# The third PSUM slot goes back to the scores early in the second stretch, and one projection pair moves to a shared bank

## The chip, the cores and the metric

The kernel runs on one core of a Trainium2 chip. The metric is the device time of one execution, in microseconds. Three runs of the kernel before gave a median of 302.7 us (302.45 to 302.79). The engines are called PE (TensorE matmul), PEld (its weight loads), DVE (VectorE), ACT (ScalarE), POOL (GpSimd) and SP (the queue that issues transfers).

## The reference

One transformer layer over a sequence of 2048 rows of 128 features, in float32:

```python
x = x + attention(layernorm(x))      # 16 heads of 8, rotary embedding, causal mask, softmax, output projection
x = x + ffn(layernorm(x))            # base linear + shared low rank (16) + top 2 of 6 routed low-rank experts
```

In the attention, q, k and v come from one product with `w_qkv`; q and k are rotated (`x1*cos - x2*sin`, `x2*cos + x1*sin`), the scores are `q.k / sqrt(8)` for the keys up to the query's own row, and their softmax weights v.

## The kernel before

**Scores, exponentials, values.** The scores are made transposed (keys on partitions, queries along the free dimension), in 280 *units*. A unit is one PSUM slot of two banks (128x1024 float32), filled by four matmuls of 256 columns ("wide": two pairs of heads), four of 128 ("half": the last, diagonal key tile) or two of 512 ("full"). ACT takes the exponential of a whole unit from PSUM into one of eight buffers `pbuf` (L701), POOL masks the diagonal ones (L641), and PE multiplies a *block* of two units with the values (L1133, always 16 or 8 matmuls into the bank `po`). A block's value product stands `LAG` = 5 units behind its scores. When the last block of a group of four heads is done, DVE turns `po` into SBUF (L763, "evacuate"), and the next group's first value product waits for that (`o_free`).

**Stretches.** The queries are worked in six pieces. Units 0 to 7 are the first piece (query tiles 0, 1), units 8 to 23 the second (tiles 2, 3; four groups of wide, wide, wide, half), units 24 to 75 the third (tiles 4 to 7; 512 queries at a time), and so on. In text and code "the second stretch" is units 8 to 23.

**Side jobs.** Beside the attention of one piece, the engines prepare the next chunk of 512 rows: T (turn the normalised rows), Q and K (projections), QS and KS (the same with the halves of each head swapped, for the rotary term; only in the first chunks), V, B (sum for the bound), then the row's finish work. PE makes the products (L1149, L1155, L1161, L1184); `PRODUCTS_AT` says behind which unit each stands in PE's program. DVE takes Q and K with the cosine (L873), QS and KS with the sine (L876), adds the two (L788), and splits the sum into three bfloat16 parts (L796, L798, L805, L807) that SP stacks by DMA; `JOBS_AT` says behind which unit each stands in DVE's program. Every engine works strictly through its own written order, so an instruction that waits holds all that stand behind it on that engine.

**PSUM.** Eight banks: three slots of two banks (`ps`), `po`, and `pm`, the one bank of the side jobs. In the first two pieces the scores use only slots 0 and 1; the two banks of slot 2 serve as *spare banks* for chunk 2's Q, QS, K and KS (`SPARE_BANK`), and unit 24 is the first in slot 2. Unit u may be written once ACT has read the last unit in its slot; the first unit in the spare slot also waits until DVE has taken the last spare job:

```python
if LAST_IN_SLOT[u] is not None:
    pe.wait_ge(exp_ready, LAST_IN_SLOT[u] + 1)
if u == FIRST_IN_SPARE:
    pe.wait_ge(job_fed, FED[SPARE_READ])
```

A product job waits until DVE has taken the job before it in the same bank (`AWAITED`, through `job_fed`, which DVE raises with a small `engine_nop`, L932, behind the whole job). Two side products are read by ACT instead of DVE: T of chunk 2 (L671) and V of chunk 2 (L673), each placed in ACT's order behind the exponential of the unit in `ACT_PLACES`.

**PE's order around the change (before):** unit 8, values of block 1, **V**; unit 9, **K**; unit 10, block 2; unit 11, **KS**; unit 12, block 3; unit 13; unit 14, block 4; unit 15; unit 16, block 5; unit 17; unit 18, block 6; unit 19; unit 20, block 7, **B**; unit 21; unit 22, block 8; unit 23; unit 24, block 9. Blocks 4, 6, 8 and 10 are the first of their group, and blocks 3, 5, 7 and 9 the last of one. **DVE's order:** evacuate block 1, Q, QS, first split of Q, evacuate block 2 (in the first piece each group is a single block), second split of Q, evacuate block 3, K, KS, evacuate block 5, bound (L812 to L817), first split of K, evacuate block 7, flag (L821, L822), second split of K, evacuate block 9, evacuate block 11, and then the normalisation of chunk 3's rows, behind which PE's T of chunk 3 stands. Before unit 24, PE also loads a flag and branches on it (`row_maxima`, whose body did not run here).

Of the kernel before, what the change touches and what calls it, by code (L numbers as in the profile page):

```python
# [71 lines left out]
NS = 3  # L72
NS_SMALL = 2
# [25 lines left out]
def plan():  # L99


    units, blocks = [], []
    for i, (t0, tiles) in enumerate(PIECES):
        for g in range(NG):
            end = (i, g) == (NPIECE - 1, NG - 1)
            work = group_work(t0, tiles, end)
            if end:
                work[-1:] = [[unit] for unit in work[-1]]
            for n, members in enumerate(work):
                mine = list(range(len(units), len(units) + len(members)))  # L110
                for kind, kt, pairs in members:
                    units.append(dict(i=i, g=g, kind=kind, kt=kt, pairs=pairs, diagonal=kt >= t0, block=len(blocks)))
                blocks.append(dict(i=i, g=g, units=mine, first=n == 0, last=n == len(work) - 1,
                                   diagonal=any(units[u]["diagonal"] for u in mine)))
    return units, blocks


UNITS, BLOCKS = plan()
MASKS_THROUGH = [sum(u["diagonal"] for u in UNITS[:n + 1]) for n in range(len(UNITS))]
FIRST_UNIT = [next(n for n, u in enumerate(UNITS) if u["i"] == i) for i in range(NPIECE)]  # L120
SLOT = [u % NS_SMALL if u < FIRST_UNIT[2] else (u - FIRST_UNIT[2] - 1) % NS for u in range(len(UNITS))]
LAST_IN_SLOT = [next((v for v in range(u - 1, -1, -1) if SLOT[v] == SLOT[u]), None) for u in range(len(UNITS))]
FIRST_IN_SPARE = SLOT.index(NS_SMALL)
NEW_KEYS_UNIT = {next(n for n, u in enumerate(UNITS) if u["i"] == i and u["diagonal"]): p for i, p in NEW_PREP.items()}
# [25 lines left out]
def value_terms(block):  # L150
# [19 lines left out]
PRODUCT_JOBS = ("T", "Q", "QS", "K", "KS", "B", "V", "O", "X", "R", "U", "F")  # L170
INPUT_OF = {"T": "L3", "Q": "T", "K": "T", "V": "T", "B": "BD", "O": "A", "X": "M3", "R": "X", "U": "W2", "F": "U"}
READ_BY_ACT = (("T", 2), ("V", 2))
SPARE_BANK = {("Q", 2): 0, ("QS", 2): 1, ("K", 2): 0, ("KS", 2): 1}

LATE_FILLS = ([("Q", 0.0, 2 * TC + t) for t in range(TC)]
              + [("K", ONE_ONE, 3 * TC + t) for t in range(TC)] + [("Q", 0.0, 3 * TC + t) for t in range(TC)])
# [30 lines left out]

SMALL_PRODUCTS = (
    (("T", 2), ("Q", 2), ("B", 1), ("QS", 2)),
    (("V", 2), ("K", 2), ("KS", 2), ("B", 2)),  # L210
)
SMALL_PLACES = (
    (2, 4, 4, 7),
    (0, 1, 3, 12),
)
ACT_PLACES = (2, 9)
POOL_STACK_PLACE = 5


# [29 lines left out]
PRODUCTS_AT, PRODUCTS = products()  # L249
COPIES_AT = dict(zip(ACT_PLACES, READ_BY_ACT))  # L250
FULL = {job: sum(other not in READ_BY_ACT for other in PRODUCTS[:n + 1]) for n, job in enumerate(PRODUCTS)}


def awaited(job):


    name, c = job
    mine = SPARE_BANK.get(job)
    before = [other for other in PRODUCTS[:PRODUCTS.index(job)] if SPARE_BANK.get(other) == mine]
    needs = before[-1:] + ([(INPUT_OF[name], c)] if name in INPUT_OF else [])  # L260
    return max((JOB[need] for need in needs if need in JOB), default=None)


AWAITED = {job: awaited(job) for job in PRODUCTS}
SPARE_READ = max(JOB[job] for job in SPARE_BANK)
FEEDS = sorted({n for n in AWAITED.values() if n is not None} | {SPARE_READ})
# [3 lines left out]
def build(nc, x, w_qkv, rope_c, rope_s, w_out, w_down, w_up, w_base, router_b, ident, head_sum,  # L270
# [3 lines left out]
    with ExitStack() as ctx:  # L274
# [232 lines left out]
        def product_bank(name, c):  # L507

            spare = SPARE_BANK.get((name, c))
            return pm[:, :] if spare is None else ps[:, NS_SMALL, spare, :]  # L510
# [135 lines left out]
        def _(act):  # L646
# [47 lines left out]
            for u, unit in enumerate(UNITS):  # L694
                act.wait_ge(scores_ready, u + 1)
                if u >= NPB:
# [3 lines left out]
                probs = pbuf[:, u % NPB, :].rearrange("p (b q) -> p b q", b=2)  # L700
                nc.scalar.activation(probs[:, :, 0:width], ps[:, SLOT[u], :, 0:width],  # L701
                                     ACT.Exp, scale=SCALE).then_inc(exp_ready, 1)
# [392 lines left out]
        def _(pe):  # L1095
            def scores(u):
# [7 lines left out]
                for at, pair in enumerate(unit["pairs"]):  # L1104
                    for dk, q0, n, place in pieces(unit["kind"]):
# [3 lines left out]
                        for e in range(2):  # L1109
                            ins = nc.tensor.matmul(ps[:, SLOT[u], e, place:place + n],  # L1110
                                                   side(kst, e)[:, g * 2 + pair, key:key + P],
# [51 lines left out]
            def job(name, c):  # L1163

                if AWAITED[name, c] is not None:
                    pe.wait_ge(job_fed, FED[AWAITED[name, c]])
                product = product_bank(name, c)
                tile = lambda t: slice(t * P, (t + 1) * P)
                nt = FINISHES[c][1] if name in FINISH else TC
                if (name, c) == ("Q", 2):  # L1170
                    pe.wait_ge(second_read, 1)
                if (name, c) in (("QS", 2), ("K", 2)):
                    pe.wait_ge(second_read, 2)
                if name in ("Q", "QS", "K", "KS", "V") and c == 2:
                    pe.wait_ge(second_input, 1)
                if (name, c) == ("B", 1):
                    pe.wait_ge(second_input, 1)
                if (name, c) == ("B", 2):
                    pe.wait_ge(v_ready, 3)
                if name == "T":  # L1180
                    if c == 2:
                        pe.wait_ge(second_rows, TC)
                    for t in range(TC):
                        ins = nc.tensor.transpose(product[:, tile(t)], xn[:, chunk(c) % 2, t, :], idf[:, :])  # L1184
                elif name in ("K", "KS", "Q", "QS"):
                    ins = project(c, name, product)
                elif name == "V":
                    ins = project_v(c, product)
                elif name == "B":
                    ins = sum_bound(product)  # L1190
                elif name == "O":
                    pe.wait_ge(ffn_in, 16 * 5)
                    for t in range(nt):
                        ins = nc.tensor.matmul(product[:, tile(t)], feat[:, tile(t)], wout[:, :], start=True, stop=True)  # L1194
                elif name == "X":
                    for t in range(nt):
                        ins = nc.tensor.transpose(product[:, tile(t)], ln[:, t, :], idf[:, :])
                elif name == "R":
                    for t in range(nt):
                        ins = nc.tensor.matmul(product[:, t * P:t * P + RD + E], feat[:, tile(t)], wdown[:, :],  # L1200
                                               start=True, stop=True)
                elif name == "U":
                    for t in range(nt):
                        ins = nc.tensor.transpose(product[0:RD + 1, tile(t)], low_rank[:, t, 0:RD + 1], idf[:, :])  # L1204
                elif name == "F":
                    base(product, nt)
                    for t in range(nt):
                        ins = nc.tensor.matmul(product[:, tile(t)], lowT[0:RD + 1, t, :], wup[:, :], start=False, stop=True,  # L1208
                                               skip_group_check=True)
                ins.then_inc(act_full if (name, c) in READ_BY_ACT else job_full, 1)  # L1210
# [183 lines left out]
```

## Time and profile before

| | |
|---|---|
| median of 3 runs | 302.7 us (302.45 to 302.79) |
| profiled execution | 302.73 us, span 301.0 us |
| PE busy | 279.7 us, 93% |
| ACT busy | 267.3 us, 89% |
| DVE busy | 140.5 us, 47% |
| POOL busy | 65.9 us, 22% |
| granted TensorE clock | 1.00 throughout |

The profiled execution took 302.73 us, of which 301.0 us are the span from its first to its last instruction; about 1.7 us lie around it. The busy shares are averages over stages; which engine holds up which, in the stage of the change, has to be read from the order in time.

### The profile page before, as it was taken

The page shows a single profiled execution, that of the slowest core. Times are in us where ns is not written, and L with a number is a line of the kernel's source. Part 1 is how long each engine was busy: PE and PEld are TensorE (multiplying, and loading weights), DVE is VectorE, ACT ScalarE, POOL GpSimd, SP SyncE. Part 2 cuts the span into 40 slices and gives each one's busy share as a digit, 9 for nine tenths or more (in the row PEclk, how much of TensorE's full clock was granted, in tenths as well). Part 3 has the DMA queues.
Part 4 walks back from the last instruction along what each step waited for, and adds up shares of the span by engine and source line. Part 5 has one row for each costly group of instructions (what it writes and reads, how often), then busy time and mean ns, then how long its engine had stood idle before and what let it go on. Part 6 is the DMA issues. An engine that isn't in the chain of part 4 may idle for free.

```text
span 301.0 us, 7509 instructions
## 1 busy us (share of the span) xinstructions
PE 279.7 (93%) x3002; PEld 101.6 (34%) x3002; DVE 140.5 (47%) x422; ACT 267.3 (89%) x302; POOL 65.9 (22%) x144
## 2 busy tenths in 40 slices
PE   7969989998999899899999999999999999999995
PEld 2624332223334122132224124433533334433342
DVE  5876866688754767728421005551001514101064
ACT  8557899898997989999999999999999999999900
POOL 3576465413303004003030030101101010103000
PEclk9999999999999999999999999999999999999999
DMA  6343433006500100610000000000100000000000
GB/s 198 113 106 86 126 106 108 0 3 165 152 0 2 38 1 5 162 47 0 3 0 18 20 2 2 2 2 2 35 3 3 2 2 0 2 20 2 3 0 17
DMA packets 15256, 11.75 MB, mean 39 GB/s; under 512 B 2081, under 2 KB 14226, under 8 KB 15218
## 3 DMA queue, kind: packets, MB, share of 16 engines
q1 hardware_dynamic: 14594, 10.64, 12.8%
q8 instruction: 25, 0.41, 0.6%
q0 software_dynamic: 192, 0.39, 0.5%
q10 hardware_dynamic: 432, 0.20, 0.3%
q14 instruction: 13, 0.11, 0.1%
HBM read 3.88 MB, written 1.05 MB: 16 GB/s over the span
## 4 chain that ended last, share of the span: by engine, by line
PE 35%; ACT 27%; issue 16%; DVE 16%; DMA 2%; SPq 0%; ACTq 0%; DVEq 0%
ACT pbuf L701 27%; PE po L1133 16%; PE ps L1110 9%; DVE rest L781 3%; PE ps L1149 2%; PE pm L1149 1%; DMA qst<-parts 1%; DVE absmax L812 1%; PE pm L1143 1%; PE pm L1194 1%; PE pm L1155 1%; DMA xs<-x_dram 1%; DVE rot L775 1%; DVE rest L798 1%; PE pm L1208 1%
## 5 line engine op out<-in xcount | busy, mean ns | idle before, releaser
L701 ACT ACTIVATE pbuf<-ps 128x1024 f32<-128x1024 f32 (+1 forms) x280 | 254.0, 1092 | 15.0 <-PE ps L1110 14.3
L1133 PE MATMUL po<-pbuf,va 128*9 128x256 f32 (+3 forms) x1792 | 143.8, 426 | 2.6 <-ACT pbuf L701 1.4
L1110 PE MATMUL ps<-qst,kst 64*128 64x256 bf16 (+3 forms) x896 | 97.1, 297 | 7.5 <-ACT pbuf L701 3.6
L641 POOL TENSOR_SCALAR_AFFINE_SELECT pbuf<-pbuf 128x256 f32<-128x256 f32 (+1 forms) x104 | 48.2, 486 | 199.7 <-ACT pbuf L701 199.1
L1110 PEld LDWEIGHTS ps<-qst,kst 64*128 64x128 bf16 x896 | 29.6, 94 | 102.9 <-ACT pbuf L701 78.3
L1133 PEld LDWEIGHTS po<-pbuf,va 128*9 128x9 f32 x1792 | 35.2, 89 | 57.6 <-issue 35.8
L763 DVE STREAM_TRANSPOSE oq<-po 128x256 f32<-128x256 f32 (+1 forms) x24 | 12.9, 538 | 83.3 <-PE po L1133 83.0
L1256 PE MATMUL ps<-kst 128*128 128x512 bf16 x46 | 11.3, 380 | 1.0 <-issue 1.0
L781 DVE TENSOR_TENSOR rest<-pm,sinT 32x512 f32<-32x512 f32 x16 | 11.0, 687 | 0.3
L730 DVE BATCH_NORM_STATS2 stats<-xs 128x6 f32<-128x128 f32 x32 | 7.1, 281 | 3.2 <-DMA xs<-x_dram 1.7
L1149 PE MATMUL ps<-xnT,wqkv 128*128 128x256 f32 (+1 forms) x24 | 8.3, 470 | 0.2 <-ACT xnT L671 0.2
L926 DVE COPY lowT<-pm 113x512 f32<-113x512 f32 (+1 forms) x4 | 2.5, 624 | 12.5 <-PE pm L1204 12.5
L929 DVE TENSOR_TENSOR xs<-pm,xs 128x512 f32<-128x512 f32 (+1 forms) x4 | 2.5, 625 | 11.8 <-PE pm L1208 11.8
L1256 PE MATMUL ps<-xnT 128*128 128x512 bf16 x16 | 5.6, 530 | 1.5 <-DVE xnT L1044 1.5
L899 DVE TENSOR_TENSOR xs<-pm,xs 128x512 f32<-128x512 f32 (+1 forms) x4 | 2.5, 625 | 9.4 <-PE pm L1194 9.4
L1256 PEld LDWEIGHTS ps<-kst 128*128 128x128 bf16 x46 | 4.3, 99 | 5.6 <-issue 1.9
L600 POOL MEMSET qst<- 128x512 f32 (+1 forms) x9 | 6.0, 692 | 0.0
L788 DVE TENSOR_TENSOR rot<-rot,rest 128x512 f32<-128x512 f32 (+1 forms) x10 | 5.9, 585 | 0.3
L798 DVE TENSOR_TENSOR rest<-rot,parts 128x512 f32<-128x512 f32 (+1 forms) x8 | 5.6, 702 | 0.3
L649 ACT COPY kst<-fillers 128x2048 f32<-128x2048 f32 x3 | 5.7, 1897 | 0.0
L775 DVE TENSOR_TENSOR rot<-pm,cosT 128x512 f32<-128x512 f32 x4 | 2.8, 692 | 6.0 <-PE pm L1149 5.1
L807 DVE TENSOR_TENSOR parts<-rest,parts 128x512 bf16<-128x512 f32 (+1 forms) x8 | 5.2, 645 | 0.3
(154 smaller groups left out, 178.7 us busy)
## 6 DMA issues: line engine op xcount, KB each, us to landing
qst<-parts SPq DMA_DIRECT2D x18, 128.0 KB, 2.5
kst<-parts SPq DMA_DIRECT2D x18, 128.0 KB, 2.5
xs<-x_dram SPq DMA_DIRECT2D x4, 256.0 KB, 3.8
cosT<-rope_c_dram SPq DMA_DIRECT2D x3, 256.0 KB, 4.0
sinT<-rope_s_dram SPq DMA_DIRECT2D x3, 256.0 KB, 5.0
out_dram<-xs SPq DMA_DIRECT2D x3, 256.0 KB, 2.3
kst<-parts SPq DMA_DIRECT2D x8, 64.0 KB, 2.2
qst<-parts SPq DMA_DIRECT2D x7, 64.0 KB, 2.5
```

Of the source, the lines that this page charges most:

```text
L600: nc.gpsimd.memset(stacked[:, :, first * P:(first + tiles) * P].bitcast(F32), value).then_inc(filled_by_pool, 1)
L641: ins = nc.gpsimd.affine_select(out=edge, in_=edge, compare_op=ALU.is_ge, fill=0.0, base=0, pattern=[[0, edge.shape[1]], [1, P]], channel_ ...
L701: nc.scalar.activation(probs[:, :, 0:width], ps[:, SLOT[u], :, 0:width], ACT.Exp, scale=SCALE).then_inc(exp_ready, 1)
L730: ins = nc.vector.bn_stats(stats[:, t, :], xs[:, tile + t, :])
L763: nc.vector.transpose(oq[:, g, mine, :].rearrange("p b r -> p (b r)"), po[:, 0:nt * P]).then_inc(o_free, 1)
L781: ins = nc.vector.tensor_tensor(rest[there:there + HALF, which, cols], product[here:here + HALF, :], sinT[here:here + HALF, c % 2, cols], ...
L788: return nc.vector.tensor_tensor(rot[:, which, cols], rot[:, which, cols], rest[:, which, cols], ALU.add)
L798: then(nc.vector.tensor_tensor(rest[:, which, cols], rot[:, which, cols], parts[:, which, 0, cols], ALU.subtract))
L1110: ins = nc.tensor.matmul(ps[:, SLOT[u], e, place:place + n], side(kst, e)[:, g * 2 + pair, key:key + P], side(qst, e)[:, g * 2 + pair, q:q ...
L1133: ins = nc.tensor.matmul(po[32 * j:32 * j + DH + 1, q0:q0 + n], va[:, kt, g * GH + j, :], pbuf[:, u % NPB, at:at + n], start=blk["first"] ...
L1149: return nc.tensor.matmul(product, wqkv[:, which, :], xnT[:, chunk(p) % 2, local(p)], start=True, stop=True)
L1256: nc.tensor.matmul(into, left, right, start=True, stop=True)
```

## The change

Slot 2 serves the scores from unit 10 on instead of unit 24, and so the rotation over three slots begins 14 units earlier. Of the spare banks only Q and QS remain; K and KS of chunk 2 go through `pm`, the bank that T, B and V use too, one after the other. In PE's order K stays behind unit 9, KS goes from behind unit 11 to behind unit 14, and V from behind unit 8 to behind unit 18. ACT's copy of V moves from behind the exponential of unit 9 to behind that of unit 18. DVE's order is untouched.

```diff
-SLOT = [u % NS_SMALL if u < FIRST_UNIT[2] else (u - FIRST_UNIT[2] - 1) % NS for u in range(len(UNITS))]
+BACK = FIRST_UNIT[1] + 2
+SLOT = [u % NS_SMALL if u < BACK else (u - BACK - 1) % NS for u in range(len(UNITS))]
...
-SPARE_BANK = {("Q", 2): 0, ("QS", 2): 1, ("K", 2): 0, ("KS", 2): 1}
+SPARE_BANK = {("Q", 2): 0, ("QS", 2): 1}
...
 SMALL_PRODUCTS = (
     (("T", 2), ("Q", 2), ("B", 1), ("QS", 2)),
-    (("V", 2), ("K", 2), ("KS", 2), ("B", 2)),
+    (("K", 2), ("KS", 2), ("V", 2), ("B", 2)),
 )
 SMALL_PLACES = (
     (2, 4, 4, 7),
-    (0, 1, 3, 12),
+    (1, 6, 10, 12),
 )
-ACT_PLACES = (2, 9)
+ACT_PLACES = (2, 18)
...
                 if (name, c) == ("Q", 2):
                     pe.wait_ge(second_read, 1)
-                if (name, c) in (("QS", 2), ("K", 2)):
+                if (name, c) == ("QS", 2):
                     pe.wait_ge(second_read, 2)
```

Through the tables, unit 10 (`FIRST_IN_SPARE`) now waits for DVE to have taken QS (`SPARE_READ`), K waits for DVE's flag job of chunk 1, KS for DVE's K, and V for DVE's KS. The last 256 units rotate over the three slots as before, one step shifted.

## Rows read from the trace of the kernel before

**Rows 1.** The page: busy time, then shares of the chain that ended last.
```profile
PE 279.7 (93%) x3002; PEld 101.6 (34%) x3002; DVE 140.5 (47%) x422; ACT 267.3 (89%) x302; POOL 65.9 (22%) x144
...
PE 35%; ACT 27%; issue 16%; DVE 16%; DMA 2%; SPq 0%; ACTq 0%; DVEq 0%
```
**Rows 2.** ACT in order of time, units 9 to 36: start, duration, count, idle before.
```profile
28.59 1.02 ACT L701 ACTIVATE pbuf<-ps 128x1024 f32<-128x1024 f32 x1 [1.16 <-PE ps L1110]
29.51 0.58 ACT L673 COPY va<-pm 128x512 f32<-128x512 f32 x1
29.98 1.58 ACT L701 ACTIVATE pbuf<-ps 128x1024 f32<-128x1024 f32 x2
32.35 10.61 ACT L701 ACTIVATE pbuf<-ps 128x1024 f32<-128x1024 f32 x12 [0.78 <-PE ps L1110]
43.15 12.24 ACT L701 ACTIVATE pbuf<-ps 128x1024 f32<-128x1024 f32 x13 [0.19 <-PE ps L1110]
```
**Rows 3.** PE in order of time, from V behind unit 8 to T of chunk 3.
```profile
27.07 1.16 PE L1155 MATMUL pm<-wqkv,xnT 128*128 128x128 f32 x8
28.16 0.39 PE L1110 MATMUL ps<-qst,kst 64*128 64x256 bf16 x4
...
29.55 0.39 PE L1110 MATMUL ps<-qst,kst 64*128 64x256 bf16 x4
...
30.86 1.13 PE L1149 MATMUL ps<-xnT,wqkv 128*128 128x512 f32 x2
31.91 0.39 PE L1110 MATMUL ps<-qst,kst 64*128 64x256 bf16 x4
...
33.75 1.05 PE L1133 MATMUL po<-pbuf,va 128*9 128x256 f32 x16
34.74 0.29 PE L1110 MATMUL ps<-qst,kst 64*128 64x128 bf16 x4
35.44 0.39 PE L1110 MATMUL ps<-qst,kst 64*128 64x256 bf16 x4 [0.41 <-ACT pbuf L701]
...
37.27 1.05 PE L1133 MATMUL po<-pbuf,va 128*9 128x256 f32 x16
...
38.95 0.39 PE L1110 MATMUL ps<-qst,kst 64*128 64x256 bf16 x4 [0.41 <-ACT pbuf L701]
...
41.05 1.05 PE L1133 MATMUL po<-pbuf,va 128*9 128x256 f32 x16 [0.20 <-DVE oq L763]
...
42.73 0.39 PE L1110 MATMUL ps<-qst,kst 64*128 64x512 bf16 x2 [0.40 <-issue]
...
53.34 0.66 PE L1184 MATMUL pm<-idf,xn 128*128 128x128 f32 x4 [0.82 <-DVEq L932]
```
**Rows 4.** DVE in order of time, from the evacuation of block 1 to that of block 11.
```profile
27.21 0.45 DVE L763 STREAM_TRANSPOSE oq<-po 128x256 f32<-128x256 f32 x1 [1.20 <-PE po L1133]
...
29.14 0.69 DVE L788 TENSOR_TENSOR rot<-rot,rest 128x512 f32<-128x512 f32 x1
...
33.14 0.45 DVE L763 STREAM_TRANSPOSE oq<-po 128x256 f32<-128x256 f32 x1
33.63 0.69 DVE L873 TENSOR_TENSOR rot<-ps,cosT 128x512 f32<-128x512 f32 x1
34.35 0.69 DVE L876 TENSOR_TENSOR rest<-ps,sinT 128x512 f32<-128x512 f32 x1
...
36.66 0.45 DVE L763 STREAM_TRANSPOSE oq<-po 128x256 f32<-128x256 f32 x1 [0.90 <-PE po L1133]
...
40.46 0.45 DVE L763 STREAM_TRANSPOSE oq<-po 128x256 f32<-128x256 f32 x1
...
47.05 0.45 DVE L763 STREAM_TRANSPOSE oq<-po 128x256 f32<-128x256 f32 x1 [2.64 <-PE po L1133]
```
**Rows 5.** Busy time by engine in two windows: PE, PEld, DVE, ACT, POOL, granted clock, DMA.
```profile
27.07:33.75 6.68, 6.65 (x72) 2.92 (x68) 6.05 (x11) 4.68 (x7) 2.87 (x7) 1.00 0.37 92
33.75:42.73 8.98, 7.52 (x121) 2.96 (x120) 7.14 (x14) 8.82 (x11) 3.84 (x7) 1.00 0.40 107
```

## The prediction

> **What bounds the kernel now.** I read the page first. PE is busy for 93% of the span and ACT for 89%, and the chain that ended last passes through PE (35%), ACT (27%) and DVE (16%) [rows 1]. No single engine is the bound, so the question for each microsecond is which hand-over ends last in the stretch that the change touches. The change touches units 9 to 24 only; behind unit 24 the same three-slot rotation runs in both kernels. So I read the timelines of ACT, PE and DVE from 27 to 54 us, side by side, and placed each matmul group in the program by counting units and blocks.
>
> The ACT timeline tempts one to see a slot problem. ACT starts unit 9 after 1.16 us of idle time and unit 12 (at 32.35) after 0.78 us, then runs twelve and thirteen exponentials almost without a gap [rows 2]. The PE timeline shows waits for a slot too: 0.41 us before unit 16 (35.44) and 0.41 us before unit 20 (38.95), both released by an exponential [rows 3].
>
> The PE timeline also shows why ACT idled earlier. From 27.07 to 33.75 PE is busy for 6.65 of 6.68 us [rows 5]: V stands between units 8 and 9, K between 9 and 10, KS between 11 and 12. Those idle times of ACT are not a lack of slots. They are PE's side jobs.
>
> DVE is the third reader. From the evacuation of block 1 at 27.21 to the end of KS's sine product at 34.35 + 0.69 = 35.04 it is all but unbroken (6.05 of the first 6.68 us [rows 5], and no row of it begins with a wait for PE after the first) [rows 4]: Q, QS, the first split of Q, evacuation of block 2, the second split, evacuation of block 3 (33.14), K, KS. Nothing in that row of work waits on what the change moves, except KS at its end. So **the evacuation of block 3 stays at 33.14 in either kernel**, and so does the earliest start of block 4's value product, the first of the next group: 33.14 + 0.45 = 33.59, plus the hand-over. What the hand-over from an evacuation to PE costs shows at block 8: that of block 7 ends at 40.46 + 0.45 = 40.91 [rows 4], and PE, which waited for it, starts at 41.05 [rows 3], 0.14 us later. That gives 33.73. Before, block 4 started at 33.75 [rows 3]. PE reached it just as DVE allowed it.
>
> **The change part by part, as a pinned point and a sum behind it.**
>
> *Ahead of 33.75.* V leaves the place behind unit 8 (start to start 28.16 − 27.07 = 1.09 us) and KS the place behind unit 11 (31.91 − 30.86 = 1.05 us) [rows 3]. PE gets 2.14 us free there. Unit 9 starts 1.09 us sooner, at about 27.1, and K ends at about 28.5. Then comes the added wait: unit 10 needs slot 2, which DVE gives back when QS is added up and the small instruction behind it has run. The addition ends at 29.14 + 0.69 = 29.83 [rows 4]; a hand-over by that instruction is about as long as the 0.14 us above. So unit 10 starts at about 29.95 to 30.0, against 29.55 before: **1.4 us of new waiting on PE, and unit 10 is 0.4 us later than now**. Behind the waiting unit stand the value product of block 2 and unit 11, all 0.4 us late. With KS gone from there, unit 12 follows unit 10 by 31.91 − 29.55 − 1.05 = 1.31 us [rows 3] and starts at about 31.3, 0.6 us sooner. Blocks 3 and 4 then wait for the evacuations of blocks 2 and 3, and block 4 starts at 33.73. All of the 2.14 us is spent in waits for DVE: 1.4 us at unit 10 and the remaining 0.7 us at those two blocks. The gain at the pinned point is nothing.
>
> *ACT ahead of that point.* ACT may start unit 12 about 0.4 us sooner (31.9 instead of 32.35 [rows 2]). It does not last, because unit 15 stands behind KS.
>
> *From 33.75 to unit 24.* Before, this took 42.73 − 33.75 = 8.98 us, of which PE was busy for 7.52 [rows 5], so 1.46 us were idle. Of these, 0.40 us before unit 24 is the flag and its branch ("issue" [rows 3]); it stays. The rest, 1.06 us, is what later work can fill: 0.41 + 0.41 + 0.20 us of listed waits [rows 3] and crumbs. Into this window come KS (behind unit 14) and V (behind unit 18): 1.05 + 1.09 = 2.14 us. So unit 24 is late by 2.14 − 1.06 = **1.08 us**.
>
> *What else waits in that window.* KS needs DVE to have read K: 33.63 + 0.69 = 34.32 [rows 4], plus the hand-over, before block 4 ends at 34.74; no wait. DVE now waits for KS's product: it ends at about 35.8 (34.74 + 1.05), so the sine product starts 1.5 us later than 34.35, and the addition, as long as that at 29.14 (0.69 us [rows 4]), ends at about 37.3. The evacuation of block 5 is queued behind it: 37.3 to 37.8 instead of 36.66 to 37.1. Block 6's product waits for that, until about 37.9. PE by itself gets there at 35.8 + (37.27 − 34.74 − 0.41) = 37.9 as well [rows 3]. Value taken: 0.05 us, between 0 (DVE in time) and 0.4 (the sine product, the addition and the evacuation each a little longer than its row). The first split of K, the flag and the second split of K stand behind that evacuation on DVE, late by as much as PE is.
>
> *ACT's copy of V.* At 29.51 it cost nothing: it ended about when unit 10's scores were ready (29.98) [rows 2]. Now ACT reaches it behind unit 18's exponential, at about 39.4, but V's product ends only near 40.0. ACT waits about 0.6 us, copies for 0.5 us (29.98 − 29.51), and starts unit 19 at about 40.6. From there to unit 24 it needs two halves and three full exponentials: three at 0.90 to 0.94 us (12.24 us for thirteen [rows 2]) and two at about 0.6 us (a full and a half one took 1.58 us from 29.98), so it could start unit 24 at about 44.6. PE gives unit 24 at 43.9 + 0.4 = 44.3. So ACT would be 1.4 us late at unit 24, PE and DVE 1.1. ACT's surplus is worked off if PE or DVE sets the next point. In the trace of before that point is T of chunk 3 at 53.34, for which PE waited 0.82 us on DVE [rows 3], and DVE's work for it starts with the evacuation of block 11 at 47.05, which waited 2.64 us for PE [rows 4]. So the chain goes PE, DVE, PE, and ACT's lag is covered.
>
> *The third slot itself.* Before, it would have been worth the two waits of 0.41 us. In the changed order PE arrives at units 16 and 20 later than their slots come free even with two slots, because KS and V stand ahead of them. I count it at nothing beyond the 1.06 us already filled.
>
> *Sum.* 0 ahead of the pinned point, +2.14 for KS and V, −1.06 for idle time filled, +0.05 for block 6's wait: about **+1.1 us** at unit 24, carried by PE and DVE into everything behind it. The profiled execution took 302.73 us against a median of 302.7, so the sum may be set on either: 302.7 + 1.1 = **303.8 us**. The case's own range is 303.4 to 304.0.
>
> The Trainium skill (Perfetto Trace Analysis, section Matmuls under Optimizing Tensor Performance) says that independent matmul groups should rotate through different PSUM banks, so that the evacuation of one overlaps the next one's matmuls. By that rule K and KS in one bank should cost a wait. Here the row of K's read on DVE says that this costs nothing while KS stands behind block 4; what costs is where it stands.
>
> **The rivals.**
>
> *Faster: the slots were what mattered (302.1 us).* If ACT's own pace set the end of the window, the third slot would let it run at that pace. Twelve exponentials took 10.61 us, 3.54 us for each group of four [rows 2]; three full ones at 0.94 us and a half at 0.6 us are 3.42 us or less, some 0.12 to 0.2 us less for each of three groups. With unit 12 0.45 us sooner and the copy of V 0.5 us in ACT's way the net is 0.3 to 0.6 us. For it speaks that ACT is busy for 8.82 of 8.98 us in that window [rows 5]. Against it: it holds only from the point where PE can take 2.14 us more work in a window in which it idles 1.06 us. The Trainium skill (Perfetto Trace Analysis, section Optimization Strategy) says that the same gap, repeated, can mean that there isn't enough PSUM; by that rule the two gaps of 0.41 us ask for this very slot, and it would come out faster. The trace agrees that the gaps are slot waits, but they are what hides half of the moved work.
>
> *About the same: the delay is absorbed behind unit 24 (302.2 to 303.3, say 302.9).* PE's score pairs wait for slots again from 47 us on, and ACT runs thirteen exponentials unbroken from 43.15 [rows 2]. If ACT's own backlog, rather than its start, set T of chunk 3, part of 1.1 us would vanish; likewise if two hand-overs ahead of it had slack. Against it: unit 24's exponential waited 0.19 us for PE [rows 2], and DVE's chain to T starts with a wait for PE. The moment PE slips, all three slip.
>
> *Slower still: ACT carries its lag on (304.1 to 304.6, say 304.2).* If V's product comes later than I reckon, or T doesn't cover ACT's 1.4 us, the copy is in the chain in full.
>
> **How the numbers follow.** The forecast's case has 0.50, the absorbed one 0.19, the faster one 0.13, the one still slower 0.18. What a measurement of this kernel can tell from no change is about 0.2%, 0.6 us. The absorbed case falls mostly within that, a small part of it below or above. So: faster 0.12, same 0.18, slower 0.70. From 302.6 to 304.4 the range holds the forecast's case, most of the slower one and most of the absorbed one, a little over 0.8.
>
> **What the changed profile would show.** On PE: unit 9 near 27.1, then a gap of about 1.4 us released by DVE before unit 10 at 29.9 to 30.0; block 4 still at 33.7 to 33.8 with a wait for the evacuation; no waits of 0.41 us for exponentials before units 16 and 20; unit 24 near 43.9. On DVE: the evacuation of block 3 unchanged at 33.1, a wait of about 1.5 us for KS's product, that of block 11 at about 48.2. On ACT: about 1.2 us of idle time before unit 15 and some 0.6 before the copy of V. T of chunk 3 would be near 54.5. The prediction is wrong if block 4 starts well before 33.7, which means that DVE was not the pin, or if unit 24 is late by 1.1 us and the gap between the kernels closes later.

## The result and the profile after

The changed kernel takes **304.11 us** (median of 8 runs, 303.45 to 304.98) against 302.51 us for the kernel before (8 runs, 302.28 to 302.97). The ratio is 1.0052 with a 95% interval of 1.0035 to 1.0068, so it is slower by 0.5%, about 1.6 us. The forecast was 303.8 us, in a range of 302.6 to 304.4.

The profiled execution took 304.20 us with a span of 302.5 us. Its first exponential starts at 19.02 us, against 19.12 before. The profiled executions of this document differ by half a microsecond either way at that point (18.55 to 19.69), ahead of anything the edits touch. So below "late" and "early" mean: against the kernel before, once the start of unit 0's exponential is made equal in both.

PE in order of time, start, duration, count and idle time before, the rows that answer to [rows 3]:

```profile
26.96 0.39 PE L1111 MATMUL ps<-qst,kst 64*128 64x256 bf16 x4
27.28 1.12 PE L1150 MATMUL pm<-xnT,wqkv 128*128 128x512 f32 x2
29.92 0.39 PE L1111 MATMUL ps<-qst,kst 64*128 64x256 bf16 x4 [1.51 <-DVEq L933]
...
31.82 0.84 PE L1134 MATMUL po<-pbuf,va 128*9 128x256 f32 x16 [0.30 <-DVE oq L764]
...
33.67 1.05 PE L1134 MATMUL po<-pbuf,va 128*9 128x256 f32 x16 [0.47 <-DVE oq L764]
34.65 1.13 PE L1150 MATMUL pm<-xnT,wqkv 128*128 128x512 f32 x2
...
37.87 1.05 PE L1134 MATMUL po<-pbuf,va 128*9 128x256 f32 x16 [0.34 <-DVE oq L764]
38.85 1.16 PE L1156 MATMUL pm<-wqkv,xnT 128*128 128x128 f32 x8
...
41.95 1.05 PE L1134 MATMUL po<-pbuf,va 128*9 128x256 f32 x16 [0.17 <-DVE oq L764]
...
43.71 0.39 PE L1111 MATMUL ps<-qst,kst 64*128 64x512 bf16 x2 [0.49 <-issue]
...
54.80 0.65 PE L1185 MATMUL pm<-idf,xn 128*128 128x128 f32 x4 [1.29 <-DVEq L933]
```

Unit 9 starts at 26.96 and is 1.10 us early, and K follows; then PE stands idle for 1.51 us until DVE has given slot 2 back (29.92). Block 4's product, at 33.67, has waited 0.47 us for the evacuation of block 3: the pinned point is where it was (33.75 before). The two 0.41 us waits for a slot are gone, and KS (34.65) and V (38.85) stand in their place. Block 6's product (37.87) now waits 0.34 us for the evacuation of block 5. Unit 24 starts at 43.71 instead of 42.73, which with the 0.10 us of the start is **1.08 us late** (1.09 in the unrounded times).

DVE, the rows that answer to [rows 4]:

```profile
33.09 0.44 DVE L764 STREAM_TRANSPOSE oq<-po 128x256 f32<-128x256 f32 x1
33.56 0.69 DVE L874 TENSOR_TENSOR rot<-pm,cosT 128x512 f32<-128x512 f32 x1
35.82 0.69 DVE L877 TENSOR_TENSOR rest<-pm,sinT 128x512 f32<-128x512 f32 x1 [1.56 <-PE pm L1150]
...
37.28 0.45 DVE L764 STREAM_TRANSPOSE oq<-po 128x256 f32<-128x256 f32 x1
...
41.35 0.45 DVE L764 STREAM_TRANSPOSE oq<-po 128x256 f32<-128x256 f32 x1 [0.26 <-PE po L1134]
...
48.17 0.45 DVE L764 STREAM_TRANSPOSE oq<-po 128x256 f32<-128x256 f32 x1 [2.78 <-PE po L1134]
```

ACT, the rows that answer to [rows 2]:

```profile
36.04 3.35 ACT L702 ACTIVATE pbuf<-ps 128x512 f32<-128x512 f32 x4 [1.07 <-PE ps L1111]
40.05 0.59 ACT L674 COPY va<-pm 128x512 f32<-128x512 f32 x1 [0.66 <-PE pm L1156]
40.53 14.90 ACT L702 ACTIVATE pbuf<-ps 128x512 f32<-128x512 f32 x17
```

The windows that answer to [rows 5] (PE, PEld, DVE, ACT, POOL busy, clock, DMA):

```profile
27.00:33.67 6.67, 4.39 (x62) 1.80 (x59) 5.98 (x11) 4.50 (x6) 3.29 (x7) 1.00 0.48 125
33.67:43.71 10.04, 9.03 (x129) 4.44 (x129) 7.21 (x14) 8.30 (x11) 3.19 (x6) 1.00 0.31 82
```

Ahead of the pinned point PE is now busy for 4.39 of 6.67 us; 2.26 us of work have left and nothing has come sooner for it. Behind it PE is busy for 9.03 us where it was 7.52. ACT has no idle time between its copy of V and T of chunk 3 (seventeen exponentials in one row, from 40.53): it reaches unit 24 at its own pace, 1.16 us late, just behind PE.

Behind unit 24 a second, smaller loss appears. T of chunk 3 starts at 54.80 instead of 53.34, so it is 1.56 us late. From there to the last exponential nothing is gained or lost.

### The profile page after: what moved, and what is told of

It is laid out like the page before. It is cut to its first block, busy times and chain, and to the rows that moved or that the text cites. A ratio compares the mean times of both kernels' runs of the same rounds, so it can differ in the third digit from the quotient of the medians.

```text
span 302.5 us, 7509 instructions
## 1 busy us (share of the span) xinstructions
PE 278.9 (92%) x3002; PEld 102.0 (34%) x3002; DVE 141.2 (47%) x422; ACT 267.0 (88%) x302; POOL 66.1 (22%) x144
## 3 DMA queue, kind: packets, MB, share of 16 engines
HBM read 3.88 MB, written 1.05 MB: 16 GB/s over the span
## 4 chain that ended last, share of the span: by engine, by line
PE 34%; ACT 27%; issue 16%; DVE 16%; DMA 3%; POOL 1%; SPq 1%; ACTq 0%; DVEq 0%; POOLq 0%
ACT pbuf L702 27%; PE po L1134 16%; PE ps L1111 9%; DVE rest L782 3%; PE pm L1150 2%; DMA xs<-x_dram 2%; DVE rot L789 1%; DMA kst<-parts 1%; DVE oq L764 1%; PE pm L1195 1%; PE pm L1156 1%; PE pm L1144 1%; PE pm L1209 1%; DVE absmax L813 1%; DVE stats L731 1%
## 5 line engine op out<-in xcount | busy, mean ns | idle before, releaser
L1111 PE MATMUL ps<-qst,kst 64*128 64x256 bf16 (+3 forms) x896 | 95.8, 297 | 8.0 <-ACT pbuf L702 2.8
L1150 PE MATMUL pm<-xnT,wqkv 128*128 128x512 f32 x12 | 6.8, 645 | 0.2 <-DVEq L933 0.2
L1150 PE MATMUL ps<-xnT,wqkv 128*128 128x256 f32 (+1 forms) x20 | 6.1, 434 | 0.2 <-ACT xnT L672 0.2
```

What stands on the lines that cost most here:

```text
L1111: ins = nc.tensor.matmul(ps[:, SLOT[u], e, place:place + n], side(kst, e)[:, g * 2 + pair, key:key + P], side(qst, e)[:, g * 2 + pair, q:q ...
L1150: return nc.tensor.matmul(product, wqkv[:, which, :], xnT[:, chunk(p) % 2, local(p)], start=True, stop=True)
```

## The experiments

This table holds, for each profiled execution, how late PE's first matmul of unit 24, the exponential of unit 24 and the last exponential (unit 279) start (counted from the unrounded trace), and the times of all runs. Where ACT's figure for unit 24 is the later one, ACT was behind PE there. Ratios are to runs of the kernel before on the same chips.

| run | unit 24, PE | unit 24, ACT | last | median us (lowest to highest, runs) | ratio (interval) |
|---|---|---|---|---|---|
| changed kernel | +1.09 | +1.16 | +1.58 | 304.11 (303.45 to 304.98, 8) | 1.0052 (1.0035 to 1.0068) |
| after_again | +1.09 | +1.16 | +1.98 | 304.46 (303.67 to 305.43, 6) | 1.0057 (1.0041 to 1.0072) |
| after_warm | +0.94 | +1.16 | +1.00 | 303.76 (303.15 to 304.12, 5) | 1.0032 (1.0020 to 1.0044) |
| moves_only | +2.80 | +2.80 | +2.82 | 305.09 (304.0 to 306.11, 6) | 1.0074 (1.0051 to 1.0098) |
| slot_at_18 | −0.15 | −0.15 | −0.10 | 302.46 (302.07 to 303.88, 12) | 0.9997 (0.9985 to 1.0010) |
| before_v_late | +0.98 | +0.98 | +1.89 | 304.36 (303.18 to 306.26, 9) | 1.0051 (1.0031 to 1.0072) |
| v_back | +0.93 | +0.93 | +0.95 | 303.80 (303.23 to 304.38, 6) | 1.0038 (1.0025 to 1.0051) |
| v_back_swap | −0.08 | +0.20 | +0.69 | 304.80 (303.31 to 307.37, 6) | 1.0077 (1.0041 to 1.0112) |
| v_back_swap_x | −0.08 | +0.21 | +0.29 | 302.78 (302.31 to 303.54, 12) | 1.0006 (0.9997 to 1.0016) |
| after_swap_x | +0.86 | +1.16 | +1.22 | 303.62 (303.4 to 303.9, 5) | 1.0035 (1.0022 to 1.0049) |
| slot18_swap | −1.15 | −0.71 | +2.21 | 302.67 (301.96 to 305.05, 6) | 1.0014 (0.9985 to 1.0044) |
| slot18_swap_x | −1.14 | −0.71 | −1.17 | 301.85 (301.23 to 302.21, 12) | 0.9970 (0.9957 to 0.9983) |
| reordered_x | −1.78 | −1.35 | −1.29 | 301.41 (300.66 to 302.67, 12) | 0.9958 (0.9946 to 0.9970) |

**The moves without the slot.** The changed kernel, scores on two slots to unit 23:

```diff
-SLOT = [u % NS_SMALL if u < BACK else (u - BACK - 1) % NS for u in range(len(UNITS))]
+SLOT = [u % NS_SMALL if u < FIRST_UNIT[2] else (u - FIRST_UNIT[2] - 1) % NS for u in range(len(UNITS))]
```

> The changed kernel with the scores kept on two slots up to unit 23 (slot 2 idle from QS to unit 24); K, KS and V stand where the change puts them. Theory of the prediction (the moved products cost, the third slot is worth nothing there): unit 24 starts 1.1 us later than in the kernel before, as in the changed one, 303.6 to 304.1 us. Theory that the third slot hides part of the moved work: PE waits for slots at units 18, 20 and 22 again, unit 24 is late by about 1.7 us, 304.3 to 304.9 us. Rival that the slot itself hurts (its wait before unit 10 is what costs): with that wait gone unit 24 is late by under 0.5 us, 302.9 us.

Unit 24 was 2.80 us late, more than any theory had it. The profile shows two things: waits for a slot, as the second theory has it, and a stretch at half the clock. From the timeline of PE in this run, then its windows (the granted clock is the third number from the end):

```profile
31.56 1.07 PE L1133 MATMUL po<-pbuf,va 128*9 128x256 f32 x16 [1.66 <-POOL pbuf L641]
...
33.52 1.90 PE L1133 MATMUL po<-pbuf,va 128*9 128x256 f32 x16
...
42.89 0.39 PE L1110 MATMUL ps<-qst,kst 64*128 64x256 bf16 x4 [0.52 <-ACT pbuf L701]
```
```profile
29.00:31.00 2.00, 0.76 (x16) 0.23 (x8) 1.72 (x4) 1.96 (x3) 1.48 (x2) 1.00 0.28 69
31.00:33.00 2.00, 1.44 (x22) 0.73 (x24) 1.86 (x4) 0.00 (x0) 0.55 (x2) 0.76 0.70 184
33.00:35.00 2.00, 2.00 (x22) 0.56 (x18) 0.81 (x2) 1.79 (x2) 0.00 (x0) 0.50 0.52 140
35.00:37.00 2.00, 2.00 (x18) 0.67 (x18) 0.46 (x1) 0.38 (x2) 0.63 (x1) 0.89 0.38 109
```

PE had idled 1.66 us ahead of block 3, and then block 4's product took 1.90 us at a granted clock of 0.50 (1.2 GHz) instead of 1.05 at 1.00. Four of this kernel's six executions had a mean clock of 0.992; the two at 1.000 took 304.0 and 304.1 us. An estimate of what the clock took: the evacuation of block 3 ends at 33.12 and its hand-over takes 0.14 us, so block 4 could have started at 33.26; at the full clock it and KS behind it take 0.98 + 1.06 = 2.04 us, to 35.30, and the next scores started at 36.44. That is about 1.1 us of the 2.80, and the 1.7 us left are the second theory's number. The times don't confirm it: the two executions at full clock are within 0.3 us of the changed kernel's ten (median 303.88). So whether the third slot hides some of the moved work in this order stays open.

**The slot without the moves.** The kernel before, slot 2 back at unit 18:

```diff
-SLOT = [u % NS_SMALL if u < FIRST_UNIT[2] else (u - FIRST_UNIT[2] - 1) % NS for u in range(len(UNITS))]
+BACK = 18
+SLOT = [u % NS_SMALL if u < BACK else (u - BACK - 1) % NS for u in range(len(UNITS))]
```

> The kernel before with one edit: slot 2 returns at unit 18, after KS has been taken from it; no product moves. Theory that DVE pins block 8 (the evacuation of block 7 stands behind the first split of K on DVE): PE's 0.41 us wait before unit 20 goes, block 8 still starts at 41.0 to 41.1, unit 24 at 42.7, time unchanged at 302.5 us. Rival that slots were what mattered: unit 24 and the total are 0.4 us earlier, 302.1 us.

No change (0.9985 to 1.0010). The wait before unit 20 went and came back one step on, for the evacuation of block 7. PE, then DVE:

```profile
41.63 1.05 PE L1134 MATMUL po<-pbuf,va 128*9 128x256 f32 x16 [0.98 <-DVE oq L764]
```
```profile
40.00 1.00 DVE L799 TENSOR_TENSOR rest<-rot,parts 128x512 f32<-128x512 f32 x1
41.03 0.45 DVE L764 STREAM_TRANSPOSE oq<-po 128x256 f32<-128x256 f32 x1
```

The evacuation stands right behind the split of K in DVE's order. A slot wait of 0.41 us had stood ahead of a DVE wait and hidden it. Unit 24 came only 0.15 us early in the profile, because the "issue" time ahead of it was 0.25 us here and 0.40 before.

**V alone.** The kernel before with V and its copy at unit 18:

```diff
-    (("V", 2), ("K", 2), ("KS", 2), ("B", 2)),
+    (("K", 2), ("KS", 2), ("V", 2), ("B", 2)),
...
-    (0, 1, 3, 12),
+    (1, 3, 10, 12),
...
-ACT_PLACES = (2, 9)
+ACT_PLACES = (2, 18)
```

> The kernel before with V alone moved as in the change (product behind unit 18, ACT's copy behind the exponential of unit 18), K and KS in the spare banks, two slots. Theory of a sum over moved work: block 4 stays at 33.75, V's 1.09 us meets about 0.65 us of idle time behind unit 18, and ACT's copy comes on top: unit 24 late by 0.8 to 0.9 us with ACT starting unit 19 1.2 us late, 303.4 us. Rival that only KS matters (through DVE): unit 24 late by 0.2 us or less, 302.6 us.

Unit 24 was 0.98 us late, near the 0.8 to 0.9 of the sum; block 8 was 0.77 us late, and the "issue" time before unit 24 was 0.62 us instead of 0.40. Another 0.9 us came between units 32 and 36, on the way to T of chunk 3, of which more below.

**V undone, KS still late.**

```diff
-    (("K", 2), ("KS", 2), ("V", 2), ("B", 2)),
+    (("V", 2), ("K", 2), ("KS", 2), ("B", 2)),
...
-    (1, 6, 10, 12),
+    (0, 2, 6, 12),
...
-ACT_PLACES = (2, 18)
+ACT_PLACES = (2, 9)
...
-                if (name, c) == ("B", 2):
+                if (name, c) in (("K", 2), ("B", 2)):
                     pe.wait_ge(v_ready, 3)
```

> The changed kernel with V back behind unit 8 and its copy behind the exponential of unit 9, K behind unit 10 (it now waits for ACT's copy of V out of the shared bank), KS behind unit 14, third slot from unit 10. Theory of the prediction's sum (PE's moved time is what costs): only KS's 1.05 us is left to fill 1.06 us of idle time, so unit 24 is late by 0.4 us or less, 302.6 to 302.9 us. Rival, a chain through DVE (KS late, so evacuations of blocks 5 and 7 late behind the addition, the bound and the first split of K): unit 24 is late by about 1.1 us although V is back, 303.6 us.

The theory that PE's moved time is all that costs fell here: with V's 1.09 us back in its cover, unit 24 was still 0.93 us late. PE now idled for 1.12 us ahead of block 8. The row names ACT, but ACT's last exponential was long done; the evacuation of block 7 on DVE ended at 41.17 + 0.45 = 41.62, 0.15 us ahead of PE's start. PE, then DVE:

```profile
41.77 1.05 PE L1134 MATMUL po<-pbuf,va 128*9 128x256 f32 x16 [1.12 <-ACT pbuf L702]
```
```profile
33.04 0.45 DVE L764 STREAM_TRANSPOSE oq<-po 128x256 f32<-128x256 f32 x1 [0.33 <-PE po L1134]
...
35.78 0.69 DVE L877 TENSOR_TENSOR rest<-pm,sinT 128x512 f32<-128x512 f32 x1 [1.57 <-PE pm L1150]
...
40.37 0.77 DVE L799 TENSOR_TENSOR rest<-rot,parts 128x512 f32<-128x512 f32 x1
41.17 0.45 DVE L764 STREAM_TRANSPOSE oq<-po 128x256 f32<-128x256 f32 x1
```

KS is late, so DVE idles 1.57 us; addition, evacuation of block 5, bound and the first split of K are all late behind it, and the evacuation of block 7 stands behind them, 1.19 us late. Not all of that is the changed kernel's: here K stands behind unit 10, so the evacuation of block 3 is itself 0.38 us late (0.05 in the changed kernel). In the changed kernel the evacuation of block 7 is 1.00 us late and had waited 0.26 us for PE, so DVE's chain alone would have had it 0.74 us late.

**That chain undone as well.** On top of v_back, on DVE:

```diff
-SECOND = ("Q", "QS", "Q1", "Q2", "K", "KS", "BD", "K1", "B", "K2")
+SECOND = ("Q", "QS", "Q1", "Q2", "K", "KS", "BD", "B", "K1", "K2")
...
-    (0, 1, 1, 3, 5, 6, 9, 10, 14, 15),
+    (0, 1, 1, 3, 5, 6, 9, 12, 12, 15),
```

> The kernel of the run v_back with one more edit, on DVE: the flag and the first split of K stand behind the evacuation of block 7 instead of the split ahead of it. Theory of the chain through DVE: block 8's wait for that evacuation (1.12 us in v_back) shrinks to 0.4 us or less and unit 24 is late by 0.4 us instead of 0.9 to 1.1, 303.0 us. Rival that PE's own added work sets unit 24 there: no change against v_back, 303.6 to 303.8 us.

Unit 24 was 0.20 us late, and PE's wait of 1.12 us before block 8 was 0.10: what held block 8 in v_back was DVE's order. The total got worse all the same: in the profile DVE waited 0.76 us for the next chunk's rows, and three of the six executions had a mean clock of 0.986 to 0.994 and took 305.31 to 307.37 us. The next kernel is slot_at_18 with the same edit on DVE.

> The kernel before with slot 2 back at unit 18 (as in slot_at_18, which alone changed nothing) and on DVE the flag and the first split of K behind the evacuation of block 7. Theory that slot and DVE order pin block 8 together: PE's wait before unit 20 and the one before block 8 both go, unit 24 is 0.6 to 0.7 us earlier, 301.9 to 302.1 us. Rival that ACT's pace sets unit 24: 0.2 us or less, 302.4 us.

Here unit 24 came 0.71 us early, and in the profiled execution the end came 2.21 us late. Splits of K that end later let SP issue the loads behind them later, and DVE then waited for the rows of the next chunk. DVE, PE and the windows of slot18_swap:

```profile
49.10 0.87 DVE L731 BATCH_NORM_STATS2 stats<-xs 128x6 f32<-128x128 f32 x4 [1.16 <-DMA xs<-x_dram]
```
```profile
54.31 0.66 PE L1185 MATMUL pm<-idf,xn 128*128 128x128 f32 x4 [2.56 <-DVEq L933]
...
55.39 1.90 PE L1134 MATMUL po<-pbuf,va 128*9 128x512 f32 x8
```
```profile
51.50:55.00 3.50, 0.94 (x10) 0.52 (x8) 2.53 (x9) 2.17 (x3) 3.23 (x8) 1.00 0.00 0
55.00:57.00 2.00, 2.00 (x12) 0.14 (x10) 0.69 (x1) 1.02 (x1) 0.41 (x1) 0.50 0.00 0
57.00:59.00 2.00, 2.00 (x8) 0.62 (x6) 0.04 (x1) 0.00 (x0) 0.23 (x1) 0.65 0.00 0
```

One late load cost DVE 1.16 us and PE a wait of 2.56 us, and a stretch at half clock came behind it. The six executions fall in two groups: three with a mean clock of 0.994 took 303.31 to 305.05 us, three at 0.997 or more took 301.96 to 302.03, so their median says little. The following kernels therefore also load the rows ahead of the stacking on SP, an edit of one line. slot18_swap_x and v_back_swap_x are the two kernels above with it; after_swap_x is the changed kernel with it and the edit on DVE:

```diff
+            load_rows(2)
             stack(2)
-            load_rows(2)
```

> The kernel of slot18_swap, with one more edit on SP: the rows of the next chunk are loaded ahead of the stacking of chunk 2 instead of behind it. In slot18_swap unit 24 came 0.7 us sooner, but DVE then waited 1.16 us for those rows, T of chunk 3 came late and PE's wait of 2.56 us for it was followed by a stretch at the lower clock. Theory that the late load took the gain away: DVE has no such wait, T of chunk 3 is 0.6 to 0.9 us earlier than in the kernel before, 301.6 to 301.9 us. Rival that the stretch behind unit 24 gives the gain back in another way: 302.3 us or more.

0.9970 (0.9957 to 0.9983). With the load in time, the slot (put where no product has to move for it) and the order on DVE together gain 0.8 us. What that order and the load would gain without the slot was not run.

> The kernel of v_back_swap (the changed kernel with V back behind unit 8, K behind unit 10, and DVE's flag and first split of K behind the evacuation of block 7) with the rows loaded ahead of the stacking. Theory that with both chains undone only crumbs of the change's loss are left: unit 24 late by 0.1 to 0.4 us as in v_back_swap (0.2), no wait of DVE for rows, 302.6 to 303.0 us; the wait ahead of unit 10 (1.5 us) now and then costs the clock. Rival that the slot from unit 10 is a loss by itself: 303.3 us or more.

1.0006 (0.9997 to 1.0016): V back in its place, DVE's order changed, the third slot from unit 10 on, and the time is that of the kernel before. That doesn't show the slot at unit 10 to be free. slot18_swap_x has the same order on DVE and the same load, and there they gain; against it, this kernel is 0.9 us later at unit 24 (+0.21 against −0.71) and 0.9 us slower (302.78 against 301.85). K and KS late in the shared bank, with the slot from unit 10, still cost that much, and the edits on DVE and SP pay it back. Which of the two, the slot or the products, takes it was not separated.

> The changed kernel with only the chain through DVE undone: the flag and the first split of K behind the evacuation of block 7, rows loaded ahead of the stacking; V stays behind unit 18. Theory that either chain alone holds unit 24 back (PE's moved products here, DVE's late evacuation in v_back): unit 24 late by 1.1 to 1.2 us as in the changed kernel, 303.7 to 304.2 us. Rival that DVE's chain is the whole cause: unit 24 late by 0.2 us as in v_back_swap, 302.8 us.

The exponential of unit 24 was 1.16 us late, as in the changed kernel, but PE was not: its block 8 was 0.93 us late (1.00 in the changed kernel) and its unit 24 was 0.86 (1.09), of which 0.17 is a shorter "issue" time. What holds the exponential at 1.16 is ACT, which waits for the late V and then has no gap. PE, then ACT:

```profile
41.65 1.05 PE L1134 MATMUL po<-pbuf,va 128*9 128x256 f32 x16
...
43.24 0.39 PE L1111 MATMUL ps<-qst,kst 64*128 64x512 bf16 x2 [0.33 <-issue]
```
```profile
39.82 0.59 ACT L674 COPY va<-pm 128x512 f32<-128x512 f32 x1 [0.66 <-PE pm L1156]
40.30 14.84 ACT L702 ACTIVATE pbuf<-ps 128x512 f32<-128x512 f32 x17
```

So with DVE's chain undone, PE's moved products still make PE 0.9 us late, and ACT's wait for V makes ACT 1.16 us late.

**The idle time filled.** Is the clock part of the changed kernel's loss? Ten matmuls in the wait before unit 10:

```diff
-FEEDS = sorted({n for n in AWAITED.values() if n is not None} | {SPARE_READ})
+FEEDS = sorted({n for n in AWAITED.values() if n is not None} | {SPARE_READ, JOB["Q", 2]})
...
+                if u == FIRST_IN_SPARE:
+                    pe.wait_ge(job_fed, FED[JOB["Q", 2]])
+                    keep_warm(10, kst[:, 0, 0:P], kst[:, 0, 0:2 * P], ps[:, NS_SMALL, 0, 0:2 * P])
```

> The changed kernel once more, beside the next one. Its first eight times lay between 303.45 and 304.98 us, and two of the three highest had a mean granted clock of 0.992 or 0.994. Expected: 304.1 us again, with some executions at a clock below 0.996, and these the slowest.

> The changed kernel with ten matmuls of 256 columns put into PE's wait ahead of unit 10 (on keys that are long there, into the bank from which DVE has read Q, after it has). They add no result and leave the order alone; the wait for QS stays as long. Theory that PE's idle time there now and then costs it the full clock: all executions show a granted clock of 0.996 or more, the highest times go, the median falls by 0.2 to 0.6 us to 303.5 to 303.9 us. Rival that the clock has no part: the same median and spread as the changed kernel beside it.

The changed kernel beside it took 304.46 us; of its fourteen executions in all, four had a mean clock of 0.992 or 0.994, and they took 304.56, 304.65, 304.98 and 305.43 us. With the wait filled, five executions all showed 0.998 or more and none took over 304.12 us. PE in that run:

```profile
28.50 1.26 PE L1257 MATMUL ps<-kst 128*128 128x256 bf16 x10
30.04 0.40 PE L1111 MATMUL ps<-qst,kst 64*128 64x256 bf16 x4 [0.28 <-DVEq L933]
```

The exponential of unit 24 was 1.16 us late as ever, and block 8 1.00, so the order in which work waits is the same up to there. The lower clock is gone from all five executions. What that is worth in time is not clear of noise: 1.0032 (1.0020 to 1.0044) against 1.0057 (1.0041 to 1.0072) beside it and 1.0052 (1.0035 to 1.0068) before, and the ten executions of the changed kernel at 0.999 or more had a median of 303.88 us, close to the 303.76 here.

**The order that follows from it.** The kernel before with slot 2 back at unit 18, V behind unit 9, K behind 10, KS behind 13, the rows loaded ahead of the stacking, and on DVE K ahead of the second split of Q, and the flag and the first split of K behind the evacuation of block 7 (the lines for slot and load are those shown above):

```diff
-SECOND = ("Q", "QS", "Q1", "Q2", "K", "KS", "BD", "K1", "B", "K2")
+SECOND = ("Q", "QS", "Q1", "K", "Q2", "KS", "BD", "B", "K1", "K2")
...
-    (0, 1, 1, 3, 5, 6, 9, 10, 14, 15),
+    (0, 0, 2, 3, 6, 6, 8, 13, 13, 14),
...
-    (0, 1, 3, 12),
+    (1, 2, 5, 12),
...
-ACT_PLACES = (2, 9)
+ACT_PLACES = (2, 10)
```

> The kernel before, reordered around its waits: slot 2 back at unit 18, V behind unit 9, K behind unit 10, KS behind unit 13 (K and KS still in the spare banks), DVE takes K ahead of the second split of Q, the flag and the first split of K stand behind the evacuation of block 7, rows loaded ahead of the stacking. Theory (a replay of the order with the durations of the rows): unit 24 and T of chunk 3 are 0.9 to 1.2 us earlier, 301.4 to 301.8 us. Rival that ACT's pace and the evacuations leave nothing: 302.3 us or more.

301.41 us, 0.9958 (0.9946 to 0.9970), faster than both kernels by 1.2 and 2.7 us. KS, at 31.73 us, fits ahead of block 4's product, which starts at 33.11 and, with its start made equal, 0.16 us sooner than before. From its PE timeline:

```profile
31.73 1.12 PE L1150 MATMUL ps<-xnT,wqkv 128*128 128x512 f32 x2
...
33.11 1.05 PE L1134 MATMUL po<-pbuf,va 128*9 128x256 f32 x16
```

## Why the prediction was right, and where not

*The pinned point.* Right. Evacuation of block 3 at 33.09 (forecast 33.14), block 4 at 33.67 (33.73), both with the waits named: 1.51 us before unit 10 (forecast 1.4), then 0.30 and 0.47 us.

*The sum to unit 24.* Right in size: 1.08 us late on PE against 1.08 plus 0.05. KS and V took 1.06 and 1.09 us (34.65 to 35.71, 38.85 to 39.94). The other terms were off and cancelled, which is luck. From start to start, units 15 and 16 took 0.44 us instead of 1.02, units 19 and 20 0.43 instead of 1.03 and units 21 and 22 0.78 instead of 0.98: 1.38 us of waiting filled, not 1.06. Against that stands block 6's wait: units 17 and 18 ahead of it took 0.95 us instead of 0.74, so it cost 0.21 and not 0.05 (the row shows 0.34 us of idle time). And the "issue" time before unit 24, which "stays" in the prediction, was 0.49 instead of 0.40; over all runs it lay between 0.13 and 0.62, and no run shows why. DVE's wait for KS was 1.56 us (forecast 1.5), ACT's waits 1.07 and 0.66 us (1.2 and 0.6).

*What causes it.* Right for the changed kernel, but the prediction saw only a part of what stands beside it. It put the delay down to PE's work moved out of its cover and gave KS's way through DVE 0.05 us. PE's path is the one that ends last in the changed kernel: the evacuation of block 7 waited 0.26 us for PE there, and with DVE's order changed (after_swap_x) PE's block 8 is still 0.93 us late instead of 1.00. V alone makes unit 24 0.98 us late (before_v_late). Close behind PE run two more chains. DVE's evacuations behind a late KS would have block 8 about 0.74 us late (1.00 less 0.26), and in v_back, where K and KS are read later still, they make unit 24 0.93 us late (0.20 when the DVE order is changed). ACT, behind the late V, is 1.16 us late at unit 24 in both kernels. The three give 1.1 to 1.2 us, not the sum, because they run side by side. The step that failed is "the first split of K, the flag and the second split of K stand behind that evacuation on DVE, late by as much as PE is": I followed DVE to the evacuation of block 5 and not on to that of block 7. It did no harm to the number, because PE's path was 0.26 us longer.

*The third slot counted at nothing.* Not settled for units 11 to 23 of the changed order: moves_only lost much more in its profile, but with the lower clock in it. Less an estimate for the clock it would be 1.7 us late at unit 24, 0.6 more than the changed kernel, while its two executions at full clock (304.0 and 304.13 us) were within 0.3 us of the changed kernel's at full clock. In the order of before the slot alone is worth nothing (slot_at_18), as its wait hides another.

*Carried to the end.* The last exponential was 1.58 us late, not 1.1. The missing term is the way from unit 24 to T of chunk 3. PE reached block 11 late by a further 0.14 us, and DVE's chain behind it was 0.33 us longer than before. Its last rows, before and then after:

```profile
51.75 0.16 DVE L457 SCALAR_TENSOR_TENSOR rstd<-sq,rstd 128x4 f32<-128x4 f32 x1
51.94 1.29 DVE L471 TENSOR_SCALAR xn<-xs,mv,rstd 128x128 f32<-128x128 f32 x4
```
```profile
52.88 0.28 DVE L458 SCALAR_TENSOR_TENSOR rstd<-sq,rstd 128x4 f32<-128x4 f32 x1
53.20 1.49 DVE L472 TENSOR_SCALAR xn<-xs,mv,rstd 128x128 f32<-128x128 f32 x4
```

The extra between unit 24 on PE and T of chunk 3 was 0.46 us here, 0.87 in after_again and 0.06 in after_warm, all of them the same order of work, so it is not a fixed price of the change; and it is as large in before_v_late (0.87). What lengthens DVE's rows stays open. POOL's fills and masks run beside all four normalisations in both kernels (from 51.76 to 53.70 before, from 52.74 on after), so the overlap as such doesn't explain the difference; where in each row they fall may, and no edit tests it. The gap before block 11 was 0.37 us in after_again and 0.36 in before_v_late, and the profile puts it down to "issue", with nothing it waits for; its cause stays open too.

*The rivals.* "Faster" needed PE to absorb 2.14 us of work, which it couldn't. The Trainium skill (Perfetto Trace Analysis, section Optimization Strategy) reads a repeated gap as a possible lack of PSUM: slot_at_18 took one of the gaps away and the time stayed (0.9997); with DVE's order changed too, and the load ahead, the kernel was faster (0.9970). "Slower still" had ACT's lag as its mechanism; ACT was 1.16 us late at unit 24 (forecast 1.4) and 1.09 at unit 28, no more than DVE at the evacuation of block 9 (1.09), so it was covered as forecast, and the measured 304.1 us came near that rival's time for other reasons.

*The clock* was in no term. It was lower in four of fourteen executions, the profiled ones not among them. The medians of 304.11 and 304.46 us stand against 303.88 for the ten executions at full clock and 303.76 for after_warm: an estimate of 0.2 to 0.4 us, not clear of noise. The forecast of 303.8 us is 0.3 us off the median, but its step of 1.1 us is 0.5 off the measured 1.6: the kernel before took 302.51 us in these runs, not the 302.7 it was set on. Of the 0.5 us, 0.46 is the way to T in the profiled execution.

## What to carry to other kernels

When a product is moved, follow both ways on from it: the engine that makes it, and every instruction queued behind its reader, up to the next point where the first engine waits for the second. Chains that run side by side don't add up, and undoing one shows little; undo both before calling either harmless, and read each engine's own start at the point where they meet, because one engine's marker can stand still while another moves. When an edit undoes a delay, give the same edit to a kernel without the delay as well: it may be a gain of its own. A buffer that removes a wait pays only if no other wait stands right behind it, and a work item that ends later on the splitting engine may hold back a load queued on SP for a later stage.

## What the runs showed of the hardware that was not expected

Two waits of PE were followed by the lower of its clock's two levels (granted 0.50, 1.2 GHz): 1.66 us in moves_only, where a block of sixteen matmuls then took 1.90 instead of 1.05 us, and 2.56 us in slot18_swap. But other waits as long as the first were not. After 1.51 us in the profiled execution of the changed kernel, and after 1.69, 1.70 and 1.69 us before T of chunk 3 in after_again, before_v_late and v_back_swap, the clock stayed at 1.00. From after_again, the wait and the windows around it:

```profile
55.11 0.66 PE L1185 MATMUL pm<-idf,xn 128*128 128x128 f32 x4 [1.69 <-DVEq L933]
```
```profile
54.00:56.00 2.00, 0.89 (x8) 0.53 (x8) 1.20 (x5) 1.33 (x2) 2.00 (x5) 1.00 0.00 0
56.00:58.00 2.00, 2.00 (x12) 0.42 (x10) 0.49 (x1) 1.02 (x1) 1.09 (x3) 1.00 0.00 0
```

So the length of a single wait doesn't decide it in these traces. The Trainium skill (TensorE: Matmul & The Clock Gate, Part 1) says that the array's clock depends on how busy it has lately been; the trace agrees in that both falls came behind a wait of PE. A wait of this length has a price that varies from one execution to the next: the changed kernel's times spread over 1.5 us and more, those of the kernel before, but for a few executions, over 0.9 or less.
